# Feed-forward first, and attention with scores in row strips, probabilities scaled on Pool and turned in fp32, and fp32 values in column strips

## The chip, the cores and the metric

The kernel runs on one core of one Trainium2 chip. Its engines are TensorE (PE; PEld is its weight load), VectorE (DVE), ScalarE (ACT), GpSimd (Pool) and SyncE (SP, which here only issues DMAs). The metric is the device time of one execution in microseconds (us), lower is better. All times below are of this one core.

## The reference, cut to what matters

Input x is 8192 tokens of 512 numbers (fp32), in 64 blocks of 128 tokens.

```python
xn = layernorm(x)                                    # over the 512 numbers, no scale or shift
qkv = xn @ Wqkv + bqkv                               # 512 -> 1536; 16 heads of 32 numbers
scores = einsum('bhnqd,bhnkd->bhnqk', qb, kwin) / sqrt(512)   # a block sees itself and both neighbours
scores = where(|kpos - qpos| <= 128 and 0 <= kpos < 8192, scores, -1e30)
attn = softmax(scores)
attention = einsum('bhnqk,bhnkd->bhnqd', attn, vwin) @ Wout + bout
h = bitlinear(xn, w_fc) + gate * (xn @ v.T @ fast_b.T @ u.T)  # 512 -> 2048, weights rounded to -1, 0, 1 times a row scale
ffn = bitlinear(max(h, 0) ** 2, w_proj)                       # 2048 -> 512
out = x + attention + ffn
```

## The kernel before

Two stages run one after the other. `attention` writes x plus the attention result to a DRAM tensor `partial`; `feed_forward` reads x and `partial` and writes the output. Each engine has its own program, written out in a fixed order, and the engines meet at semaphores only. All loops are unrolled.

A product that must be close to fp32 is made of fp32r (rounded fp32) operands: each operand is split in a high part (a copy that rounds) and a low part (the rest), and three matmuls are added, high x high, low x high, high x low. `job_ps` holds such projections, two banks in turn.

**Attention** works on tiles of two blocks (256 tokens, 32 tiles). A tile has 32 steps (`STEPS`): c (4 groups of four heads) x b (2 blocks) x h (4 heads of the group). A step is one head of one query block against three key blocks, 128x384 scores. In step s PE makes, in this order: the scores of s (L913); a quarter of a projection, called a job (L290 for queries and keys, 256 columns each; L300 for values and L965 for the output projection, 512 columns each); the turn (transpose through PE) of the probabilities of step s-1 in three 128x128 pieces (L934), on some steps with a fourth, the rider (L931), which turns a piece of x or of the attention result; and every second step the products with the values of two earlier steps (L954, L956).

- Scores are one matmul with 96 rows: the three passes (high, high, low) of the 32 numbers of a head lie below each other in `stack`. ACT and DVE write the parts to `qk_parts` (L697 to L823), and SP copies them with 12 DMAs of 64 KB for each c (L544) to the other partitions.
- DVE adds the mask, scales and finds the maximum (`mask_scale_max`, L789). ACT takes the exponential (L716). PE turns the result, not yet divided by its sum. ACT copies the turned piece to fp16 (`pT_high`, L727), DVE makes the fp16 rest (`pT_low`, L800).
- The products with values take the turned probabilities (128x128) as weights and 97 or 65 columns of bf16 values: a column of ones for the row sum, the value's high, middle and low part. DVE adds the parts (`fold`, L813, L814), Pool multiplies by the reciprocal of the sum (L628).
- x is normalised and turned inside attention, and again in feed-forward.

**Feed-forward** first rounds, scales and turns the weights (`prepare_feed_forward`), then runs 16 tiles of 512 tokens in 16 steps: nine matmuls up (L1568 to L1572), eight down for two steps before (L1582, L1584), and on ACT and DVE relu, square, high part, low part. For the next tile it normalises x, turns it and splits it (`f_xT_hi`, `f_xT_lo`).

`prepare_attention` loads and splits the weights at the kernel's start. Between the blocks of the program all engines jump to new code and meet.

## Time and profile before

| | us |
|---|---|
| median of 3 runs | 2811.32 (2810.37 to 2813.68) |
| profiled execution, its own time | 2808.96 |
| its span, first to last instruction | 2807.0 |
| attention, up to the first DMA of feed-forward's weights | 1675.4 |
| feed-forward with its preparation | 1131.6 |

The median lies 2.36 us above the profiled execution's own time, and that lies 1.96 us above its span. An engine's busy time is the union of its instructions. A matmul's own duration contains the pipeline's depth, so what a matmul costs in a row of them is the distance from one start to the next, and not its duration; the same holds in part for ACT and DVE. PEclk 1.00 is TensorE's full clock, 2.4 GHz; 0.50 is 1.2 GHz.

### The profile page before, as it was taken

What the parts mean: (1) busy time and instruction counts of PE and PEld (TensorE: products, weight loads), DVE (VectorE), ACT (ScalarE), POOL (GpSimd) and SP (SyncE); (2) the same over time, 40 slices, a digit from 0 to 9 for tenths busy, and PEclk for the clock granted to TensorE, in tenths of its full rate; (3) what the DMA queues carried; (4) which work ended last, traced back from release to release, by engine and by line L of the source; (5) the groups of instructions that cost most, each with busy time, mean ns of one, the idle gap of its engine ahead of it and who ended that gap; (6) DMA issues with size and microseconds to landing.
All of it is one profiled execution on the core that took longest, in us unless ns stands there. A gap on an engine that the chain in (4) does not pass through costs nothing. (4 is left out here: it accounts for less than half of the span.)

```text
span 2807.0 us, 61651 instructions
## 1 busy us (share of the span) xinstructions
PE 2728.3 (97%) x20744; PEld 2397.7 (85%) x20744; DVE 2023.4 (72%) x5704; ACT 1712.8 (61%) x3745; POOL 639.1 (23%) x812
## 2 busy tenths in 40 slices
PE   6999999999999999999999977999999999999998
PEld 5899999999999999999999965888888888888887
DVE  4899999999999999999999966444444444444443
ACT  3678778787787877878778756333333333333332
POOL 3223323233233332323323220111111111111111
PEclk9999999999999999999999987999999999999999
DMA  3333333333333333333333333111111111111101
GB/s 114 92 97 93 99 94 105 89 92 100 95 98 96 94 99 94 99 94 94 99 95 95 97 90 137 49 46 49 45 50 46 49 46 45 46 45 46 45 31 45
DMA packets 177015, 219.98 MB, mean 78 GB/s; under 512 B 32112, under 2 KB 115280, under 8 KB 176192
## 3 DMA queue, kind: packets, MB, share of 16 engines
q1 hardware_dynamic: 175840, 215.31, 26.7%
q8 instruction: 170, 2.79, 0.4%
q14 instruction: 141, 1.16, 0.1%
q0 software_dynamic: 864, 0.73, 0.1%
HBM read 80.91 MB, written 33.55 MB: 41 GB/s over the span
## 5 line engine op out<-in xcount | busy, mean ns | idle before, releaser
L716 ACT ACTIVATE probs<-neg_scores,neg_max 128x384 f32<-128x384 f32 (+1 forms) x1024 | 630.8, 616 | 341.9 <-DVE neg_max L789 335.3
L789 DVE CUSTOM_DVE_ANT_0 neg_scores<-score_ps,mask 128x384 f32<-128x384 f32 (+1 forms) x1024 | 559.9, 547 | 109.0 <-PE score_ps L913 56.2
L1441 ACT ACTIVATE relu<-up_ps,fc_scale 128x512 f32<-128x512 f32 x256 | 176.3, 689 | 656.9 <-PE up_ps L1572 656.9
L800 DVE TENSOR_TENSOR pT_lo<-pT_ps,pT_hi 128x384 f16<-128x384 f32 (+1 forms) x1024 | 561.2, 548 | 13.5 <-ACT xT_hi L729 4.9
L1515 DVE SCALAR_TENSOR_TENSOR sq<-up_ps,relu 128x512 f32<-128x512 f32 x256 | 177.0, 691 | 536.2 <-ACT relu L1441 536.2
L934 PE MATMUL pT_ps<-ident,probs 128*128 128x128 f32 x3040 | 506.6, 275 | 12.4 <-ACT probs L716 9.8
L727 ACT CAST pT_hi<-pT_ps 128x384 f16<-128x384 f32 (+1 forms) x1024 | 470.1, 459 | 3.8 <-PE pT_ps L934 3.5
L913 PE MATMUL score_ps<-stack 96*128 96x128 f32 (+2 forms) x1536 | 448.9, 347 | 0.0
L934 PEld LDWEIGHTS pT_ps<-ident,probs 128*128 128x128 f32 x3040 | 366.0, 141 | 81.3 <-DVE oT_lo L804 12.9
L1582 PE MATMUL down_ps<-proj_T,sq_hi 128*128 128x512 f32 x1024 | 408.9, 399 | 0.3 <-DVE sq_lo L1498 0.2
L1584 PE MATMUL down_ps<-proj_T,sq_lo 128*128 128x512 f32 x1024 | 404.3, 395 | 0.0
L1568 PE MATMUL up_ps<-f_xT_hi,fc_T 128*128 128x512 f32 x1024 | 399.3, 390 | 1.4 <-DVE low L1486 1.4
L1570 PE MATMUL up_ps<-f_xT_lo,fc_T 128*128 128x512 f32 x1024 | 399.3, 390 | 0.0
L628 POOL TENSOR_TENSOR o_heads<-o_sum,o_rcp 128x128 f32<-128x128 f32 x256 | 102.3, 400 | 950.4 <-DVE o_sum L814 950.4
L290 PE MATMUL job_ps<-xT_hi,wqkv_hi 128*128 128x256 f32 x1024 | 295.5, 289 | 2.6 <-PEq L318 2.6
L954 PE MATMUL o_ps<-values,pT_hi 128*128 128x97 bf16 x3040 | 295.6, 208 | 0.2 <-DVE oT_lo L804 0.2
L956 PE MATMUL o_ps<-values,pT_lo 128*128 128x65 bf16 x3040 | 288.5, 194 | 0.0
L290 PE MATMUL job_ps<-xT_hi,wqkv_lo 128*128 128x256 f32 x1024 | 288.4, 282 | 0.0
L290 PE MATMUL job_ps<-xT_lo,wqkv_hi 128*128 128x256 f32 x1024 | 287.5, 281 | 0.0
L913 PEld LDWEIGHTS score_ps<-stack 96*128 96x128 f32 x1536 | 254.8, 193 | 0.1
L954 PEld LDWEIGHTS o_ps<-values,pT_hi 128*128 128x128 f16 x3040 | 251.5, 98 | 0.6 <-DVE oT_lo L804 0.4
L956 PEld LDWEIGHTS o_ps<-values,pT_lo 128*128 128x128 f16 x3040 | 239.0, 98 | 6.3
(165 smaller groups left out, 5186.1 us busy)
## 6 DMA issues: line engine op xcount, KB each, us to landing
stack<-qk_parts SPq DMA_DIRECT2D x1536, 64.0 KB, 2.1
x_in<-in_L_attn_x SPq DMA_DIRECT2D x64, 256.0 KB, 3.2
y<-in_L_attn_x SPq DMA_DIRECT2D x64, 256.0 KB, 3.0
partial<-y SPq DMA_DIRECT2D x64, 256.0 KB, 3.4
f_x_in<-in_L_attn_x SPq DMA_DIRECT2D x64, 256.0 KB, 2.7
part_in<-partial SPq DMA_DIRECT2D x64, 256.0 KB, 3.6
out<-f_y SPq DMA_DIRECT2D x64, 256.0 KB, 2.0
fc_in<-in_L_ffn_w_fc SPq DMA_DIRECT2D x16, 256.0 KB, 6.2
```

The lines of the kernel that those rows point to most:

```text
L290: last = nc.tensor.matmul(out, w[:, k, col:col + P], a[:, k, par, :] if is_k else own_tokens(a, par, k), start=(n == 0), stop=(n == 3 * DC ...
L716: nc.scalar.activation(probs[:, r, cols], neg_scores[:, r, cols], ACT.Exp, bias=neg_max[:, s % 4:s % 4 + 1], scale=-1.0).then_inc(probs_do ...
L727: last = nc.scalar.copy(pT_hi[:, s % 4, cols], pT_ps[:, r, cols])
L789: nc.vector.tensor_tensor_reduce(out=neg_scores[:, r, cols], in0=score_ps[:, r, cols], in1=mask[:, cols], scale=-SCORE_SCALE, scalar=3e38, ...
L800: last = nc.vector.tensor_tensor(pT_lo[:, s % 4, cols], pT_ps[:, r, cols], pT_hi[:, s % 4, cols], ALU.subtract)
L913: last = nc.tensor.matmul(score_ps[:, s % 2, (w - b) * P:(w - b + count) * P], q_cols(par, c, h, b), keys[:, at:at + count * P], start=Tru ...
L934: last = nc.tensor.transpose(pT_ps[:, r, w * P:(w + 1) * P], probs[:, r, w * P:(w + 1) * P], ident[:, :])
L954: nc.tensor.matmul(o_ps[:, g % 2, col:col + VW], pT_hi[:, r, t], v, start=(w == w0), stop=False)
L956: last = nc.tensor.matmul(o_ps[:, g % 2, col:col + 1 + 2 * DH], pT_lo[:, r, t], v[:, 0:1 + 2 * DH], start=False, stop=(w == w1 - 1))
L1568: nc.tensor.matmul(up_ps[:, s % 2, :], fc_T[:, k, cols], xT_hi[:, par, k, :], start=(k == 0), stop=False)
L1582: nc.tensor.matmul(down_ps[:, b, :], sq_hi[:, s % 2, t], proj_T[:, s, :], start=(s == 0), stop=False)
L1584: last = nc.tensor.matmul(down_ps[:, b, :], sq_lo[:, s % 2, t], proj_T[:, s, :], start=False, stop=(s == FB - 1))
```

## The change

- **Order of the stages.** `feed_forward_stage` runs first and writes x plus its result to `partial`. It also stores the turned, normalised x, high and low part, to a DRAM tensor `xT` (two DMAs of 256 KB for each block, `store_xT`). Its 14 middle tiles run in a hardware loop of seven passes instead of unrolled code. `attention_stage` then loads `xT` (four DMAs of 256 KB for each two blocks) and `partial`, and writes the output. It no longer normalises, turns or splits x.
- **Steps.** Attention now has 128 steps t (tile i, group c of four heads), each with all eight heads of two blocks. One t of the new kernel is the work of eight steps s of the old one.
- **Scores.** No `stack` and no DMAs of queries and keys. q and k, high and low, stay where the projection leaves them, four heads of 32 rows below each other. A head's three passes are three matmuls with 32 rows, placed in that head's row strip of the array (`tile_position=(h * DH, 0)`), the four heads after each other in each pass, each into its own bank of `score_ps`. Keys lie in a ring of four blocks; for every second tile a window wraps, and each pass is then two matmuls, 256 and 128 columns.
- **Softmax.** DVE still masks and finds the maximum, and writes to `probs`. ACT's exponential now also sums (`accum_out`). DVE takes four reciprocals at once, and Pool multiplies each head's 128x384 probabilities by them in place (`normalise`).
- **Turned probabilities.** PE turns as before. ACT copies each head's result to `pT` in fp32; there is no low part, so DVE has no part in it.
- **Values.** They are kept in fp32, one copy by ACT. The product takes a head's 32 columns of values as weights and the turned probabilities as moving data (fp32, 256 or 128 columns), each head in its own column strip (`tile_position=(0, h * DH)`). Its result is already turned, so the riders for the attention result go; ACT and DVE split it (`oT_high`, `oT_low`).

Core of the diff (`job_ps` now takes three jobs a step in two banks: A is the queries and keys of t+2, then the products with values of t-1, then B, values or output projection):

```diff
-def feed_forward(nc, x, partial, fast_b, w_fc, w_proj, u, v, gate, out):
+def feed_forward_stage(nc, x, fast_b, w_fc, w_proj, u, v, gate, xT_dram, partial):
...
-            for i in range(NT):
-                tile(i, i % 2)
+            tile(0, 0)
+            with eng.Fori(0, (NT - 2) // 2) as pair:
+                for n in range(2):
+                    tile(2 * pair + 1 + n, (1 + n) % 2)
+            tile(NT - 1, (NT - 1) % 2)
...
+            def store_xT(i, par):
+                for b in range(NB):
+                    sp.wait_ge(xT_done, NB * i + b + 1)
+                    settle(sp, ticks)
+                    for low, xT in enumerate((xT_hi, xT_lo)):
+                        sp.dma_start(xT_rows(xT_dram, NB * i + b, low),
+                                     xT[:, par, :, b * P:(b + 1) * P].bitcast(F32)).then_inc(xT_stored[b], 16)
...
+            def normalise(t, b):
+                i, _ = where(t)
+                cols = window(i, b)
+                pool.wait_ge(rcp_done, 2 * t + b + 1)
+                for h in range(HC):
+                    u = b * HC + h
+                    nc.gpsimd.tensor_scalar(probs[:, u, cols], probs[:, u, cols], sum_rcp[:, u:u + 1], None, ALU.mult
+                                            ).then_inc(normalised, 1)
...
+            def exp(t, b, h):
+                i, _ = where(t)
+                cols = window(i, b)
+                u = b * HC + h
+                act.wait_ge(maxed, 8 * t + u + 1)
+                nc.scalar.activation(probs[:, u, cols], probs[:, u, cols], ACT.Exp, bias=neg_max[:, u:u + 1], scale=-1.0,
+                                     accum_out=prob_sum[:, u:u + 1]).then_inc(exped, 1)
+            def copy_pT(t, b, h):
+                i, _ = where(t)
+                seen = blocks_seen(i, b)
+                first = 3 * at(i, b)
+                act.wait_ge(turned, 8 * t + b * HC + h + 1)
+                if t >= 1:
+                    act.wait_ge(pv_done, t)
+                nc.scalar.copy(pT[:, h, first + seen.start:first + seen.stop, :].rearrange("p w t -> p (w t)"),
+                               pT_ps[:, h % 2, seen.start * P:seen.stop * P]).then_inc(pT_done, 1)
...
+            def find_max(t, b):
+                i, _ = where(t)
+                cols = window(i, b)
+                dve.wait_ge(scored, 2 * t + b + 1)
+                if t >= 1:
+                    dve.wait_ge(turned, 8 * (t - 1) + HC * (b + 1))
+                for h in range(HC):
+                    u = b * HC + h
+                    nc.vector.tensor_tensor_reduce(out=probs[:, u, cols], in0=score_ps[:, h, cols], in1=mask[:, cols],
+                                                   scale=-SCORE_SCALE, scalar=3e38, op0=ALU.add, op1=ALU.min,
+                                                   accum_out=neg_max[:, u:u + 1]).then_inc(maxed, 1)
+            def invert_sums(t, b):
+                group = slice(b * HC, (b + 1) * HC)
+                dve.wait_ge(exped, 8 * t + HC * (b + 1))
+                nc.vector.reciprocal(sum_rcp[:, group], prob_sum[:, group]).then_inc(rcp_done, 1)
...
+            def scores(t, b):
+                i, c = where(t)
+                if b == 0:
+                    pe.wait_ge(qk_done, t + 1)
+                if t or b:
+                    pe.wait_ge(maxed, 8 * t + HC * b)
+                place = at(i, b)
+                for w, key, count in key_runs(i, b):
+                    for pass_ in range(PASSES):
+                        q = q_lo if pass_ == 1 else q_hi
+                        keys = k_lo if pass_ == 2 else k_hi
+                        for h in range(HC):
+                            rows = slice(h * DH, (h + 1) * DH)
+                            last = nc.tensor.matmul(
+                                score_ps[:, h, w * P:(w + count) * P], q[rows, c, place, :],
+                                keys[rows, c, key:key + count, :], start=(pass_ == 0), stop=(pass_ == PASSES - 1),
+                                tile_position=(h * DH, 0))
+                last.then_inc(scored, 1)
+            def turn_probs(t, b, h):
+                i, _ = where(t)
+                u = b * HC + h
+                n = 8 * t + u
+                if n >= 2:
+                    pe.wait_ge(pT_done, n - 1)
+                pe.wait_ge(normalised, n + 1)
+                for w in blocks_seen(i, b):
+                    last = nc.tensor.transpose(pT_ps[:, h % 2, w * P:(w + 1) * P], probs[:, u, w * P:(w + 1) * P],
+                                               ident[:, :])
+                last.then_inc(turned, 1)
+            def probs_times_values(t):
+                i, c = where(t)
+                bank = pv_bank(t)
+                wait_job_bank(pe, 3 * (t + 1) + 1)
+                if c == 0:
+                    pe.wait_ge(v_done, min(2 * i + 3, NBLK))
+                pe.wait_ge(pT_done, 8 * t + 2 * HC)
+                parts = []
+                for blk in (2 * i, 2 * i + 1):
+                    first, second = (3 * place + blk - (2 * i - 1 + at(i, place)) for place in range(2))
+                    parts.append((blk, slice(0, 2), slice(first, second + 1, second - first)))
+                for b, blk in enumerate((2 * i - 1, 2 * i + 2)):
+                    if 0 <= blk < NBLK:
+                        place = at(i, b)
+                        seen = 3 * place + 2 * b
+                        parts.append((blk, slice(place, place + 1), slice(seen, seen + 1)))
+                for n, (blk, places, seen) in enumerate(parts):
+                    for h in range(HC):
+                        head = c * HC + h
+                        strip = slice(h * DH, (h + 1) * DH)
+                        last = nc.tensor.matmul(job_ps[strip, bank, places.start * P:places.stop * P],
+                                                values[:, blk % VR, head * DH:(head + 1) * DH], pT[:, h, seen, :],
+                                                start=(n == 0), stop=(n == len(parts) - 1), tile_position=(0, h * DH))
+                last.then_inc(pv_done, 1)
...
+            for t in range(STEPS + 3):
+                if t < STEPS:
+                    scores(t, 0)
+                for part in range(QUARTERS):
+                    if 1 <= t <= STEPS:
+                        turn_probs(t - 1, 1, part)
+                    run_a(t, part)
+                if t < STEPS:
+                    scores(t, 1)
+                if 1 <= t <= STEPS:
+                    probs_times_values(t - 1)
+                for part in range(QUARTERS):
+                    if t < STEPS:
+                        turn_probs(t, 0, part)
+                    run_b(t, part)```

PE in the steady part of attention before: one step s, from its scores on, with a quarter of a query and key job and a rider. `stack` gives both operands of the scores, `o_ps` takes the products with values.

```order
L913 MATMUL score_ps<-stack 128x128
L913 MATMUL score_ps<-stack 128x256
L290 MATMUL job_ps<-xT_hi,wqkv_hi 128x256
L290 MATMUL job_ps<-xT_lo,wqkv_hi 128x256
L290 MATMUL job_ps<-xT_hi,wqkv_lo 128x256
L290 MATMUL job_ps<-xT_hi,wqkv_hi 128x256
L290 MATMUL job_ps<-xT_lo,wqkv_hi 128x256
L290 MATMUL job_ps<-xT_hi,wqkv_lo 128x256
L931 MATMUL pT_ps<-ident,o_heads 128x128
L934 MATMUL pT_ps<-ident,probs 128x128 x3
```

PE now, in the middle of a step t: the end of job A, the scores of the second block, the products with values of the step before, then the first turn of this step.

```order
L1135 MATMUL job_ps<-xT_hi,wqkv_lo 128x256
L1200 MATMUL score_ps<-k_hi,q_hi 128x384 x4
L1200 MATMUL score_ps<-k_hi,q_lo 128x384 x4
L1200 MATMUL score_ps<-k_lo,q_hi 128x384 x4
L1238 MATMUL job_ps<-pT,values 32x256 x8
L1238 MATMUL job_ps<-pT,values 32x128 x8
L1214 MATMUL pT_ps<-ident,probs 128x128 x3
L1144 MATMUL job_ps<-wqkv_hi,xT_hi 128x512
```

The scores of four heads now stand together, and the products with values are 16 instructions of 32 output rows in place of 48 with 97 and 65 columns.

ACT before, in the same part: exponential and fp16 copy in turn, two casts of riders, the projection's high parts.

```order
L716 ACTIVATE probs<-neg_scores,neg_max 128x384
L727 CAST pT_hi<-pT_ps 128x384
L729 CAST oT_hi<-pT_ps 128x128
L716 ACTIVATE probs<-neg_scores,neg_max 128x384
L727 CAST pT_hi<-pT_ps 128x384
L729 CAST oT_hi<-pT_ps 128x128
L697 ACTIVATE qk_parts<-job_ps,qk_bias 128x256
L699 ACTIVATE qk_parts<-job_ps,qk_bias 128x256
```

ACT now, from the last exponential of a step's first block on.

```order
L985 ACTIVATE probs,prob_sum<-probs,neg_max 128x384
L1011 ACTIVATE q_hi<-job_ps,qk_bias 128x256
L1014 ACTIVATE k_hi<-job_ps,qk_bias 128x256
L985 ACTIVATE probs,prob_sum<-probs,neg_max 128x384
L1003 CAST oT_hi<-job_ps 128x256
L995 COPY pT<-pT_ps 128x384
L985 ACTIVATE probs,prob_sum<-probs,neg_max 128x384
L995 COPY pT<-pT_ps 128x384
```

The copy behind an exponential is now that of a head four places back, and between a head's exponential and its copy lie DVE's reciprocal, Pool's scaling and PE's turn.

## Rows read from the trace of the kernel before

**Rows 1.** The page's busy times: us, share of the span, number of instructions.

```profile
PE 2728.3 (97%) x20744; PEld 2397.7 (85%) x20744; DVE 2023.4 (72%) x5704; ACT 1712.8 (61%) x3745; POOL 639.1 (23%) x812
```

**Rows 2.** Stretches of attention's steady part: all engines; ACT's exponentials alone.

```profile
500.00:1000.00 500.00, 498.87 (x4944) 463.02 (x4942) 463.94 (x1456) 397.47 (x936) 155.77 (x200) 1.00 0.36 96
500.00:1000.00 500.00, 197.62 (x319) 1.00 0.36 96
```

**Rows 3.** Who waited for whom from 500 to 1000: us in total, times, longest.

```profile
ACT probs L716 <- DVE neg_max L789: 100.2, 210, 1.4
PEld pT_ps L934 <- DVE oT_lo L804: 3.3, 15, 0.3
```

**Rows 4.** Timeline of PE: start us, us, line, op; one wrapped step, values behind.

```profile
805.92 0.21 PE L954 MATMUL o_ps<-values,pT_hi 128*128 128x97 bf16 x1
...
806.36 0.48 PE L913 MATMUL score_ps<-stack 96*128 96x128 f32 x2
806.67 0.40 PE L300 MATMUL job_ps<-wqkv_hi,xT_hi 128*128 128x512 f32 x1
806.91 0.39 PE L300 MATMUL job_ps<-wqkv_hi,xT_lo 128*128 128x512 f32 x1
```

**Rows 5.** The same timeline, a step with a query and key job.

```profile
812.65 0.42 PE L913 MATMUL score_ps<-stack 96*128 96x384 f32 x1
812.91 0.28 PE L290 MATMUL job_ps<-xT_hi,wqkv_hi 128*128 128x256 f32 x1
813.03 0.28 PE L290 MATMUL job_ps<-xT_lo,wqkv_hi 128*128 128x256 f32 x1
...
813.62 0.49 PE L934 MATMUL pT_ps<-ident,probs 128*128 128x128 f32 x3
813.86 0.42 PE L913 MATMUL score_ps<-stack 96*128 96x384 f32 x1
```

**Rows 6.** Timeline of PE and its weight loads: fp32 products of 512 and 128 columns; fp32r of 128.

```profile
25.85 0.19 PEld L188 LDWEIGHTS bias_ps<-wout_raw,v_bias_wide 128*128 128x128 f32 x1 [0.24 <-issue]
26.28 0.19 PEld L188 LDWEIGHTS bias_ps<-wout_raw,v_bias_wide 128*128 128x128 f32 x1 [0.24 <-issue]
1723.74 1.06 PE L1225 MATMUL scale_ps<-diagonal,ones 128*128 128x128 f32 x8
31.50 0.28 PE L379 MATMUL job_ps<-xT_hi,wqkv_hi 128*128 128x128 f32 x1
31.61 0.28 PE L379 MATMUL job_ps<-xT_lo,wqkv_hi 128*128 128x128 f32 x1
```

**Rows 7.** Timeline of ACT: attention's pair of a step; a sum's read behind an activation.

```profile
806.35 0.46 ACT L727 CAST pT_hi<-pT_ps 128x384 f16<-128x384 f32 x1
806.71 0.60 ACT L706 CAST values<-job_ps 128x512 bf16<-128x512 f32 x1
1683.41 0.19 ACT L1243 ACTIVATION_READ_ACCUMULATOR absolute<-fc_in 128x1 f32 x1
1683.50 0.67 ACT L1261 ACTIVATE fc_T<-turn_ps,neg_round 128x512 fp32r<-128x512 f32 x1
```

**Rows 8.** Groups by shape: line, engine, op, count | busy us, mean ns | idle before.

```profile
L716 ACT ACTIVATE probs<-neg_scores,neg_max 128x384 f32<-128x384 f32 x992 | 614.5, 619 | 323.0 <-DVE neg_max L789 316.5
L789 DVE CUSTOM_DVE_ANT_0 neg_scores<-score_ps,mask 128x384 f32<-128x384 f32 x992 | 546.5, 551 | 101.1 <-PE score_ps L913 50.0 <-ACT probs L716 26.9 <-issue 0.8
L642 POOL TENSOR_TENSOR y<-y,projected 128x512 f32<-128x512 f32 x64 | 82.4, 1288 | 3.1 <-ACT projected L746 3.1
L614 POOL CAST values<-v_rest 128x512 bf16<-128x512 f32 x64 | 39.9, 623 | 157.5 <-DVE v_rest L830 157.5
```

**Rows 9.** Timeline at borders: first projection, first scores, first weight DMA of feed-forward.

```profile
28.35 0.47 PE L300 MATMUL job_ps<-wqkv_hi,xT_hi 128*128 128x512 f32 x1 [1.05 <-PEq L79]
39.33 0.55 PE L290 MATMUL job_ps<-xT_hi,wqkv_hi 128*128 128x256 f32 x1 [2.64 <-PEq L318]
1675.40 7.50 SPq L1095 DMA_DIRECT2D fc_in<-in_L_ffn_w_fc  x10
```

**Rows 10.** The page's DMA issues: count, KB each, us to landing; and a burst's rate (last number, GB/s).

```profile
x_in<-in_L_attn_x SPq DMA_DIRECT2D x64, 256.0 KB, 3.2
1680.00:1700.00 20.00, 14.75 (x54) 9.70 (x55) 14.33 (x55) 15.95 (x39) 0.00 (x0) 0.50 1.02 376
```

1242 lines of the change are left out of this document (444 added, 798 removed).

## The prediction

> **What bounds the kernel now.** I read the busy times first [rows 1]: PE is busy for 97% of the span, DVE 72%, ACT 61%, Pool 23%. Then attention's steady part [rows 2]: in 500 us PE is busy for 498.9 at the full clock, DVE for 463.9 (93%), ACT for 397.5 (79%), Pool for 155.8. The 319 exponentials there are 319 old steps, so eight of them, the work of one new step t, take 500 / 319 x 8 = 12.54 us. Waits [rows 3]: ACT waits often for DVE's maxima, but for PE's weight loads the worst releaser comes to 3.3 us in 500. PE sets the pace, and attention gains only what PE gains, until another engine takes over.
>
> What the 12.54 are made of, by the distance from one start to the next. A job's matmul of 256 columns takes 0.118 (six in 0.71 [rows 5]), one of 512 takes 0.24 [rows 4]: 24 x 0.118 + 12 x 0.24 = 5.72. Turns: three in 0.24 [rows 5], eight times 1.92. Riders: four more turns, 0.32. Scores: 0.26 with one run of keys [rows 5], 0.31 with two [rows 4], half of each: 2.28. Products with values: 12 matmuls, two steps, in 0.44 [rows 4], four times 1.76. Sum 12.00; 0.54 are gaps.
>
> **What PE does per new step.** The jobs (5.72) and the 24 turns (1.92) stay. The four riders go (-0.32). Two terms have no row, since no matmul of before shares the array with another.
>
> Scores. A column costs 0.118 / 256 = 0.46 ns, so a pass of 384 columns 0.175. Lower bound: the four strips run beside each other, a block costs three passes and what a waiting start costs (0.26 - 0.175 = 0.09) and about as much on leaving the strips: 0.70, wrapped 3 x (0.118 + 0.11) + 0.19 = 0.87, the 0.11 being the distance of 128-column matmuls, whose weight loads set the pace [rows 6]. Two blocks, half of the tiles wrapped: 1.6 us. Upper bound: nothing overlaps, 12 x 0.175 + 0.1 and wrapped 12 x 0.228 + 0.1, per step 5.0. I take 1.6: neighbours in the order lie in different rows, read different partitions and write different banks.
>
> Values. An fp32 product is two loads and two matmuls: the weight loads of the 512-column one start 0.43 apart, the eight records of four 128-column ones 0.11 apart [rows 6]. A half is so 0.215 for 256 columns and 0.11 for 128. Upper bound, nothing overlaps: 8 x 0.43 + 8 x 0.22 + 0.1 = 5.3. Lower bound, four strips at once: 2 x 0.43 + 2 x 0.22 + 0.1 = 1.4. I take a value between, for a reason in the order: the two halves of a head follow each other in the same strip, so the second waits for the first, and in a queue that starts matmuls in order the next head can only begin beside that second half. Two run at a time, not four: 8 x 0.215 + 8 x 0.11 + 0.1 = 2.7.
>
> Sum: 5.72 + 1.92 + 1.6 + 2.7 = 11.94. Of the 0.54 gaps I keep 0.2 (the values' four short runs and the riders, which wait on DVE, are gone), within 0.1 to 0.54. **12.14 us** against 12.54.
>
> The Trainium skill (TensorE: Matmul & The Clock Gate, Part 3, Packing small matmuls) gives measured gains of 3.07 times for four row strips and 2.38 for three column strips. By these the two terms would be 5.0 / 3.07 = 1.6 and 5.2 / 2.38 = 2.2, the step about 11.6 us and the kernel some 2710 us, an estimate from that page. No run here shows it yet.
>
> **Does the rest keep up?** ACT: of a 0.46 copy the next start comes after 0.36 [rows 7], so I take 0.10 off each duration. Exponential 0.62 - 0.10 [rows 8], plus a sum's read that puts off the next start by 0.09 [rows 7]: 0.61, eight times 4.9. Copies 8 x 0.36 = 2.9. Query and key parts 2 x 0.38, the result's high part 0.26, half a value copy 0.25: together 9.1 us. It loses the riders' casts and x, and gains the reads. DVE: 8 x 0.48 for the maxima (0.55 [rows 8], overlapped in part), query and key rests 0.8, 0.4 for the result's rest, reciprocals 0.2, half of an output addition 0.35: 5.6 us. `pT_low`, `fold` and x go; they are beside PE's work and save nothing themselves. Pool: no row has its new operation. Bounds: one input, 512 columns, 0.62; two inputs, 1.29 [rows 8]; so 0.47 to 0.97 for 384, eight times 3.8 to 7.8, plus half of 1.29. I take 0.6, nearer to the one-input row. All are below 12.1.
>
> The chain across engines, for the second block of a step: its last exponential, a sum's read, a reciprocal (0.18), Pool (0.47 to 0.97), three hops of about 0.1, then the first turn of the next step. I lay the orders out from the start of the first block's scores. They end at 0.8, job A with the old block's turns at 4.6, the second scores at 5.4, values at 8.1, job B with turns at 12.1. DVE takes the first maxima from 1.1 to 3.1, but the second only after the rests of queries and keys, which wait for job A and for four exponentials on ACT: from 7.4. ACT's exponentials of the second block then start at 8.0 and the last ends at 11.7. The first turn of the next step is wanted at 12.9; with Pool at 0.6 it is free at 12.7, with 0.97 at 13.1. So the chain just fits: cost 0 to 0.3 us a step, 0 taken. Were PE faster, it would be the bound: with values at 1.4 the same table closes at 11.3, since ACT then runs behind PE's turns.
>
> **Outside the steady part.** Before, attention takes 1675.4 us to feed-forward's first DMA [rows 9], less 128 x 12.54: 70 fixed. Now: weights as before until 27; no x beside them, so that eight loads of 256 KB (2.1 MB at 376 GB/s, 3.2 us to landing [rows 10]) stand on the path, 8; the opening projections 48 x 0.11 + 24 x 0.24 + 48 x 0.118 = 17 with 3 of waits; last step's values, two output projections and the store 18. 73, so +3. Feed-forward's arithmetic does not change. SP there issues eight stores of x's parts more in each tile of some 66 us, 2.1 MB or 32 GB/s; attention held 96 [rows 2]. SP's next load of x stands behind those stores, issued by step 10 of 16, and is wanted in step 1 of the next tile: some 20 us. The loop's seven jumps back: jumps to new code cost PE 1.05 and 2.64 [rows 9], with engines meeting; queued matmuls may hide them. 0 to 18 us, 7 taken. The Pool and SP queues lose value carrying and 1536 stack DMAs, which nobody on PE waited for.
>
> **Sum.** 128 x (12.14 - 12.54) = -51; +3; +7. Span 2807 - 41 = 2766, plus 1.96 outside it and 2.36 to the median: **2770 us**. Gaps and bounds of these terms (11.9 to 12.5 a step, 0 to 25 outside) give 2733 to 2831 for this case.
>
> **Rivals.**
> - *All four column strips overlap too.* For: they are different columns, and each reads its own head. Against: the two halves of a head in one strip. The chain closes at 11.3: 2811 + 10 - 128 x 1.24 = 2662.
> - *One kind of strip does not overlap* (slower). Place: in the scores each matmul has its own 128-column weight load, and loads pass one at a time, 0.11 apart, as [rows 6] may be read: 12 or 24 a block, 4.2 us a step. Or the column strips run in turn, 5.3. Either gives a step of 14.7: 2811 + 10 + 128 x 2.2 = 3100. It decides from the point where scores and values together cost over 4.6 us against my 4.3.
> - *Neither overlaps.* 18.2 a step, about 3545.
> - *The chain bites.* Pool at 0.97 or longer hops, turns waiting at each step's start: 12.4 to 12.9 a step, 2803 to 2868, middle 2835.
>
> **How the numbers follow.** Forecast 0.36, full overlap 0.18, one kind not 0.27, neither 0.05, chain 0.14. A measurement tells about 0.2%, 6 us, from no change. Faster: 0.33 of the forecast's share, 0.18, 0.03 of the chain's: 0.54. Same 0.05, slower 0.41. Both signs hold much, so the forecast's own range, 2733 to 2831, stands beside the range 2662 to 3110, which leaves out "neither" and the edges.
>
> **What would show it.** Steady PE rows: starts of the four heads' score matmuls within hundredths of a us and a block in 0.7 to 0.9; values 2.7 a step, with two heads' halves beside each other; PE over 97% busy and a step 12.1. The chain shows as PE's weight loads of the turns waiting for Pool; its row is 0.47 to 0.97 long. A score block of 1.3 or more is the queue of loads. I am wrong by a lot if strips don't share the array; a little if the loop's jumps or Pool cost more.

## The result, and the profile after

The changed kernel takes 2876.8 us (2876.1 to 2879.4) where the kernel before, run beside it, takes 2811.3: a ratio of 1.0233, interval 1.0215 to 1.0251. It is slower by 65 us; 2770 were forecast. The profiled execution has a span of 2873.4 us, so 66 more than before.

The busy times of the changed kernel's page answer to [rows 1]: us, share of the span, number of instructions. Under them stand two stretches of attention's steady part, all engines (PE, PEld, DVE, ACT, POOL, then PEclk, DMA share, GB/s) and the exponentials' line alone, which answer to [rows 2].

```profile
PE 2734.9 (95%) x21264; PEld 2110.3 (73%) x21264; DVE 1276.2 (44%) x3777; ACT 1667.3 (58%) x4261; POOL 1452.6 (51%) x1234
```

```profile
1300.00:1800.00 500.00, 485.58 (x4935) 360.90 (x4934) 224.34 (x829) 369.04 (x1055) 399.96 (x326) 1.00 0.14 40
```

```profile
1300.00:2300.00 1000.00, 437.18 (x1226) 1.00 0.14 42
```

A step has eight exponentials and eight reads of their sums, so 1226 records in 1000 us are 1000 / 1226 x 16 = **13.05 us per step**, against 12.54 before and 12.14 forecast. No engine looks full: DVE fell to 45%, PE is at 97%, Pool, which had 31%, is at 80% of the stretch. PE's 97% mislead here: a matmul's modelled end covers short pauses, and the number of its records says more (4935 in 500 us at 13.05; 5554 in a version below that takes 11.56).

The rest of the span is as forecast. Rows of the border between the stages:

```profile
1130.01 1.26 POOL L456 TENSOR_TENSOR f_y<-f_y,part_in 128x512 f32<-128x512 f32 x1
...
1133.85 1.94 SPq L689 DMA_DIRECT2D w_stage<-in_L_attn_Wqkv  x4
```

Feed-forward and its border take 1133.85 us against 1131.6, and attention 2873.4 - 1133.85 = 1739.6, of which 128 x 13.05 = 1670.4 are steps and 69 are fixed (73 forecast). The whole loss is in the step.

**Where the step goes.** The groups of Pool and PE between 1300 and 2800 us (count | busy us, mean ns | idle before, releaser), and the waits between 1500 and 2500 us (us in total, times, longest), which answer to [rows 8] and [rows 3]:

```profile
L956 POOL TENSOR_SCALAR probs<-probs,sum_rcp 128x384 f32<-128x384 f32 x920 | 1128.2, 1244 | 300.1 <-DVE sum_rcp L1063 300.1
L1214 PE MATMUL pT_ps<-ident,probs 128*128 128x128 f32 x2760 | 479.0, 283 | 43.4 <-POOL probs L956 42.8
```

```profile
DVE sum_rcp L1063 <- ACT probs L985: 446.8, 153, 3.7
POOL probs L956 <- DVE sum_rcp L1063: 199.1, 153, 2.1
...
ACT pT L995 <- PE pT_ps L1214: 114.0, 77, 1.9
```

Pool's product takes 1.244 us for 384 columns, always (1240 to 1255 ns over 920 of them), above the upper bound of 0.97. Eight make 9.95 us, and half an output addition of 1.28 brings Pool to 10.6 of 13.05. The rest is in the second list: Pool stands still for DVE's reciprocals, twice a step, 199.1 us in 1000 or 2.6 a step. The timelines of Pool, ACT and DVE through one step show the ring:

```profile
1999.30 3.69 POOL L956 TENSOR_SCALAR probs<-probs,sum_rcp 128x384 f32<-128x384 f32 x3
2002.95 1.28 POOL L961 TENSOR_TENSOR y<-y,out_bias 128x512 f32<-128x512 f32 x1
2005.08 4.91 POOL L956 TENSOR_SCALAR probs<-probs,sum_rcp 128x384 f32<-128x384 f32 x4 [0.85 <-DVE sum_rcp L1063]
2011.12 2.46 POOL L956 TENSOR_SCALAR probs<-probs,sum_rcp 128x384 f32<-128x384 f32 x2 [1.13 <-DVE sum_rcp L1063]
```

```profile
2003.69 0.48 ACT L995 COPY pT<-pT_ps 128x384 f32<-128x384 f32 x1
2004.06 0.62 ACT L985 ACTIVATE probs<-probs,neg_max 128x384 f32<-128x384 f32 x1
...
2006.91 0.62 ACT L985 ACTIVATE probs<-probs,neg_max 128x384 f32<-128x384 f32 x1 [1.41 <-DVE neg_max L1056]
...
2010.09 0.64 ACT L985 ACTIVATE probs<-probs,neg_max 128x384 f32<-128x384 f32 x1
```

```profile
2005.53 0.48 DVE L1075 SCALAR_TENSOR_TENSOR q_lo<-job_ps,qk_bias,q_hi 128x256 fp32r<-128x256 f32 x1 [0.55 <-ACT k_hi L1014]
...
2006.32 0.55 DVE L1056 CUSTOM_DVE_ANT_0 probs<-score_ps,mask 128x384 f32<-128x384 f32 x1
```

Pool ends the old block's fourth head at 2002.99 (the old block is the second block of the step before). Only then can PE turn it and ACT copy it (2003.69), and only behind that copy, in ACT's order, stands the fourth exponential of the new step's first block (2004.06). Two things hang on it.

- DVE inverts the first block's four sums in one instruction (2004.80), and Pool begins that block at 2005.08: 2.09 us after it was done, in which the output addition fits on half of the steps. It ends at 2009.99.
- ACT's query and key parts stand behind the same exponential, DVE's rests wait for them (2005.53), and the second block's maxima stand behind the rests (2006.32). So ACT starts the second block's exponentials at 2006.91, one for each copy between them, and the fourth at 2010.09. The single reciprocal waits for that fourth one, and Pool begins the second block at 2011.12, 1.13 after it was free.

For Pool the step is 8 x 1.23 + 2.09 + 1.13 = 13.06. The ring that sets it is the second way: from the end of the old block's four products to the start of the second block's 8.13 us pass on PE, ACT and DVE, and the four products themselves take 4.91, together 13.04. Pool waits for itself. The first block's products lie beside this ring, with the 1.13 behind them.

**The strips**, the part of the forecast with no row, overlap at least as well as forecast. PE's timeline of one block's scores, the values and the next turn:

```profile
2004.29 0.45 PE L1200 MATMUL score_ps<-k_hi,q_hi 32*128 32x384 f32 x4
2004.57 0.34 PE L1200 MATMUL score_ps<-k_hi,q_lo 32*128 32x384 f32 x4
2004.74 0.34 PE L1200 MATMUL score_ps<-k_lo,q_hi 32*128 32x384 f32 x4
2005.01 1.51 PE L1238 MATMUL job_ps<-pT,values 128*32 128x256 f32 x32
2006.47 0.53 PE L1214 MATMUL pT_ps<-ident,probs 128*128 128x128 f32 x3
```

A block of scores takes 2005.01 - 2004.29 = 0.72, the values 1.46. Line L1238 alone in slices of 0.05 us shows how many of its records run:

```profile
2005.00:2005.05 0.05, 0.04 (x4) 1.00 0.00 0
...
2005.20:2005.25 0.05, 0.05 (x4) 1.00 0.72 287
2005.25:2005.30 0.05, 0.05 (x8) 1.00 1.47 573
```

Four records start together and the next four 0.2 us later: all four heads, half by half, side by side.

### The profile page after: what moved, and what is told of

It is laid out like the page before. It is cut to its first block, busy times and chain, and to the rows that moved or that the text cites. A ratio compares the mean times of both kernels' runs of the same rounds, so it can differ in the third digit from the quotient of the medians.

```text
span 2873.4 us, 58706 instructions
## 1 busy us (share of the span) xinstructions
PE 2734.9 (95%) x21264; PEld 2110.3 (73%) x21264; DVE 1276.2 (44%) x3777; ACT 1667.3 (58%) x4261; POOL 1452.6 (51%) x1234
## 4 chain that ended last, share of the span: by engine, by line
PE 20%; ACT 19%; issue 9%; POOL 6%; DVE 5%; SPq 0%; DMA 0%; ACTq 0%; POOLq 0%
ACT probs L985 10%; PE job_ps L1135 10%; PE pT_ps L1214 9%; POOL probs L956 6%; ACT pT L995 5%; DVE probs L1056 2%; DVE k_lo L1079 2%; ACT k_hi L1014 2%; ACT q_hi L1011 2%; ACT oT_hi L1003 1%; DVE sum_rcp L1063 1%; PE job_ps L1250 0%; PE job_ps L1153 0%; PE job_ps L1144 0%; SPq L921 0%
## 5 line engine op out<-in xcount | busy, mean ns | idle before, releaser
L956 POOL TENSOR_SCALAR probs<-probs,sum_rcp 128x384 f32<-128x384 f32 (+1 forms) x1024 | 1245.4, 1234 | 398.3 <-DVE sum_rcp L1063 398.3
L985 ACT ACTIVATE probs<-probs,neg_max 128x384 f32<-128x384 f32 (+1 forms) x1024 | 633.3, 618 | 180.0 <-DVE neg_max L1056 180.0
L995 ACT COPY pT<-pT_ps 128x384 f32<-128x384 f32 (+1 forms) x1024 | 486.6, 475 | 249.5 <-PE pT_ps L1214 199.8
L1214 PE MATMUL pT_ps<-ident,probs 128*128 128x128 f32 x3040 | 532.1, 284 | 64.1 <-POOL probs L956 60.0
L1214 PEld LDWEIGHTS pT_ps<-ident,probs 128*128 128x128 f32 x3040 | 315.7, 141 | 321.9 <-issue 244.0
L1056 DVE CUSTOM_DVE_ANT_0 probs<-score_ps,mask 128x384 f32<-128x384 f32 (+1 forms) x1024 | 504.0, 548 | 80.2 <-PE score_ps L1200 78.6
L456 POOL TENSOR_TENSOR f_y<-f_y,part_in 128x512 f32<-128x512 f32 x64 | 87.4, 1397 | 665.1 <-DVE f_y L561 665.1
L1063 DVE RECIPROCAL sum_rcp<-prob_sum 128x4 f32<-128x4 f32 x256 | 45.5, 178 | 751.5 <-ACT probs L985 751.5
L1135 PE MATMUL job_ps<-xT_hi,wqkv_hi 128*128 128x256 f32 x1024 | 330.3, 323 | 0.0
L1135 PE MATMUL job_ps<-xT_lo,wqkv_hi 128*128 128x256 f32 x1024 | 287.3, 281 | 0.0
L1135 PE MATMUL job_ps<-xT_hi,wqkv_lo 128*128 128x256 f32 x1024 | 286.4, 280 | 0.0
L637 PEld LDWEIGHTS down_ps<-proj_T,sq_hi 128*128 128x128 f32 x1024 | 193.4, 189 | 42.8 <-DVE sq_lo L553 1.1
L639 PEld LDWEIGHTS down_ps<-proj_T,sq_lo 128*128 128x128 f32 x1024 | 193.0, 188 | 43.1
L623 PEld LDWEIGHTS up_ps<-f_xT_hi,fc_T 128*128 128x128 f32 x1024 | 192.3, 188 | 43.9 <-DVE low L541 2.0
L625 PEld LDWEIGHTS up_ps<-f_xT_lo,fc_T 128*128 128x128 f32 x1024 | 192.3, 188 | 42.5
L985 ACT ACTIVATION_READ_ACCUMULATOR probs<-probs,neg_max 128x1 f32 x1024 | 199.2, 195 | 0.0
## 6 DMA issues: line engine op xcount, KB each, us to landing
xT_hi<-xT SPq DMA_DIRECT2D x66, 256.0 KB, 3.9
xT_lo<-xT SPq DMA_DIRECT2D x66, 256.0 KB, 4.4
f_x_in<-in_L_attn_x SPq DMA_DIRECT2D x64, 256.0 KB, 3.2
xT<-f_xT_hi SPq DMA_DIRECT2D x64, 256.0 KB, 2.6
xT<-f_xT_lo SPq DMA_DIRECT2D x64, 256.0 KB, 2.8
part_in<-in_L_attn_x SPq DMA_DIRECT2D x64, 256.0 KB, 3.6
partial<-f_y SPq DMA_DIRECT2D x64, 256.0 KB, 2.0
ff_in<-partial SPq DMA_DIRECT2D x64, 256.0 KB, 3.4
```

Of the source, the lines that this page charges most:

```text
L623: nc.tensor.matmul(up_ps[:, s % 2, :], fc_T[:, k, cols], xT_hi[:, par, k, :], start=(k == 0), stop=False)
L625: nc.tensor.matmul(up_ps[:, s % 2, :], fc_T[:, k, cols], xT_lo[:, par, k, :], start=False, stop=False)
L637: nc.tensor.matmul(down_ps[:, b, :], sq_hi[:, s % 2, t], proj_T[:, s, :], start=(s == 0), stop=False)
L639: last = nc.tensor.matmul(down_ps[:, b, :], sq_lo[:, s % 2, t], proj_T[:, s, :], start=False, stop=(s == FB - 1))
L956: nc.gpsimd.tensor_scalar(probs[:, u, cols], probs[:, u, cols], sum_rcp[:, u:u + 1], None, ALU.mult).then_inc(normalised, 1)
L985: nc.scalar.activation(probs[:, u, cols], probs[:, u, cols], ACT.Exp, bias=neg_max[:, u:u + 1], scale=-1.0, accum_out=prob_sum[:, u:u + 1] ...
```

## The experiments

All shorten or lengthen one thing in the changed kernel or in a version of it. A step's length is read as above, from the exponentials' records. Experiments 1, 7, 8 and 11 change what the kernel computes and have one run each; the differences read from them are far above the 0.2% by which runs of one kernel differ. The edits are shortened: conditions around calls are left out, and nested loops stand in one line.

**1. Without the scaling.** The output lacks the division by the sums.

```
-                    normalise(t, 0)
-                    normalise(t, 1)
...
-                pe.wait_ge(normalised, n + 1)
+                pe.wait_ge(exped, n + 1)
```

> The changed kernel with Pool's scaling of the probabilities left out (the turn waits for the exponential instead; the result is attention without the division by the row sum). Theory: Pool's 1.24 us instruction paces the turns, and a step is 8 x 1.23 plus Pool's two waits of 2.09 and 1.13 us, 13.03 together. Without it the chain of the prediction's table is left, 11.3 us a step, span about 2873 - 128 x 1.7 = 2655. Rival one, the orders written out on ACT and PE cost the same with a cheap scaling: a step stays above 12.5, span above 2805. Rival two, PE itself is full (its matmuls behind a turn start late): a step of 12.5 to 13, PE still 97% busy.

2682.0 us. Its stretch and its exponentials:

```profile
1300.00:1800.00 500.00, 500.00 (x5536) 415.18 (x5533) 250.54 (x934) 407.15 (x1189) 28.35 (x22) 1.00 0.16 48
```

```profile
1300.00:2300.00 1000.00, 493.47 (x1384) 1.00 0.16 48
```

16000 / 1384 = 11.56 us per step, PE never idle. The scaling costs 1.5 us a step, which is the whole loss of 0.5 and 1.0 more; PE's own work is 11.56, where the forecast had 12.14.

**2. VectorE scales instead of Pool**, four products behind each reciprocal.

```
-normalise(t, 0)
-normalise(t, 1)
...
 nc.vector.reciprocal(sum_rcp[:, group], prob_sum[:, group]).then_inc(rcp_done, 1)
+for h in range(HC):
+    nc.vector.tensor_scalar(probs[:, u, cols], probs[:, u, cols], sum_rcp[:, u:u + 1], None, ALU.mult)
```

> The changed kernel with the same scaling on DVE, right behind the four reciprocals. DVE has 5.6 us of work in a step of 13.0; the instruction should take 0.40 to 0.48 us (a 128x512 tensor_scalar with a scalar from memory took 0.487 before), so DVE has 9 us. It delays DVE's second maxima by 1.6 us at most. Theory: a step of 11.5 to 12.4, median 2680 to 2800. Rival, the chain through DVE takes over: with the second maxima at 9.0 and not 7.4 in the table the step comes to 12.9, median about 2860.

2861.1 us, ratio 1.0179 (1.0162 to 1.0196). The product takes DVE 0.42 us instead of Pool's 1.24, and it brings only 16 us. DVE's timeline:

```profile
2003.50 0.18 DVE L1060 RECIPROCAL sum_rcp<-prob_sum 128x4 f32<-128x4 f32 x1 [2.20 <-ACT probs L982]
2003.72 1.41 DVE L1065 TENSOR_SCALAR probs<-probs,sum_rcp 128x384 f32<-128x384 f32 x4
2005.04 0.68 DVE L1092 TENSOR_TENSOR y<-job_ps,ff_in 128x512 f32<-128x512 f32 x1
2005.64 0.55 DVE L1053 CUSTOM_DVE_ANT_0 probs<-score_ps,mask 128x384 f32<-128x384 f32 x1
```

The next block's maxima stand behind the four products (and an output addition), ACT's exponentials wait for the maxima, and the next reciprocal for the exponentials. DVE then idles for 2.2 us, in a step in which it is 65% busy. It is a ring again, through other stations.

**3. Pool's product in its two-input form**, the reciprocal repeated along the row.

```
-nc.gpsimd.tensor_scalar(probs[:, u, cols], probs[:, u, cols], sum_rcp[:, u:u + 1], None, ALU.mult
+nc.gpsimd.tensor_tensor(probs[:, u, cols], probs[:, u, cols],
+                        sum_rcp[:, u:u + 1].to_broadcast([P, n_]), ALU.mult
```

> The changed kernel with Pool's tensor_scalar replaced by a tensor_tensor whose second input is the reciprocal spread over the columns. The prediction's upper bound came from Pool's two-input rows, 2.5 ns a column, 0.97 us for 384; the tensor_scalar took 3.2 ns a column. If that row holds for this form, a step is 8 x 0.97 + 3.2 = 11.0 to 11.3, median about 2650 to 2690. Rival: Pool pays for the in-place work on this tile or for its neighbours DVE and ACT, whatever the instruction: 1.2 us again and no change, 2877.

2755.2 us, ratio 0.9801 (0.9785 to 0.9817): some 2% below the kernel before, by this line alone.

```profile
L957 POOL TENSOR_TENSOR probs<-probs,sum_rcp 128x384 f32<-128x384 f32 x941 | 748.6, 827 | 594.0 <-DVE sum_rcp L1065 594.0
```

With two inputs read the product takes 0.83 us, a third less than with one. The step is now 16000 / 1328 = 12.05 us. It did not reach the 2650 to 2690 expected: Pool, 58% busy, still waits, and the products behind the first no longer set the distance of the turns. PE's own order does:

```profile
2004.15 0.49 PE L1216 MATMUL pT_ps<-ident,probs 128*128 128x128 f32 x3
...
2005.18 0.49 PE L1216 MATMUL pT_ps<-ident,probs 128*128 128x128 f32 x3
```

A turn with its quarter of a job takes 1.03. So the ring is 8.13 + 0.83 + 3 x 1.03 = 12.05, an estimate from the rows of both kernels that meets the measured step.

**4. All four exponentials of the first block ahead of the old block's copies.**

```
-for h in range(HC): copy_pT(t - 1, 1, h); exp(t, 0, h)
+for h in range(HC): exp(t, 0, h)
+for h in range(HC): copy_pT(t - 1, 1, h)
```

> The changed kernel with ACT's order alone changed: the four exponentials of a step's first block ahead of the four copies of the block before, in place of turn and turn about. Theory: Pool's wait of 2.09 us between blocks is there because the last exponential stands behind a copy that waits for Pool's own last result; with it gone Pool has 8 x 1.23 + 0.64 + the other wait of 1.1 = 11.6 us a step, median about 2877 - 128 x 1.4 = 2700, Pool over 85% busy. Rival, Pool's length alone matters: a step stays at 12.8 to 13.0, since the copies now come late to PE: 2845 to 2880.

2890.8 us, ratio 1.028 (1.0263 to 1.0297), slower still, and the theory falls in this form. Two waits from 1500 to 2500 us, and ACT's first copies of one step:

```profile
DVE q_lo L1076 <- ACT k_hi L1014: 258.9, 76, 3.4
...
PE pT_ps L1215 <- ACT pT L995: 40.1, 76, 0.7
```

```profile
2009.83 0.83 ACT L995 COPY pT<-pT_ps 128x384 f32<-128x384 f32 x2
```

The longest wait is DVE's, for ACT's query and key parts (`qk_high`), which now stand behind the fourth copy; in the changed kernel it is 41.9 us in 76 times. By the chain that the profile follows back, the step's length does not come from it. That chain goes through PE: the old block's third turn waits for its first copy (the turned pieces have two banks), that copy stands behind four exponentials, they wait for the new block's first maximum (1993.71), and the next first maximum (2006.83) waits for PE's order from that third turn on. That is 13.1 us, and no product of Pool is in it. Opening one way round closed another. This is read from the trace; no run tests it.

**5. A reciprocal for each head.** Neither Pool's instruction nor any order is changed; only the wait is cut into four.

```
-dve.wait_ge(exped, 8 * t + HC * (b + 1))
-nc.vector.reciprocal(sum_rcp[:, group], prob_sum[:, group]).then_inc(rcp_done, 1)
+for u in range(b * HC, (b + 1) * HC):
+    dve.wait_ge(exped, 8 * t + u + 1)
+    nc.vector.reciprocal(sum_rcp[:, u:u + 1], prob_sum[:, u:u + 1]).then_inc(rcp_done, 1)
...
-pool.wait_ge(rcp_done, 2 * t + b + 1)
+pool.wait_ge(rcp_done, 8 * t + u + 1)     # ahead of each head's product
```

> Pool scales as in the changed kernel, 1.244 us a head, but VectorE inverts each head's sum as soon as that head's exponentials are there (four small reciprocals in a block of queries instead of one behind the fourth head), and Pool waits for each head by itself. Nothing else is changed. Theory A, it is the wait and not the length of Pool's instruction: in the changed kernel Pool stands idle for 2.1 and 1.1 us between its two blocks of four, because the last exponentials stand on ScalarE behind copies that wait for Pool itself. With the wait cut to a head, Pool works through: 8 x 1.24 + half of 1.28 = 10.6 us per step, less than TensorE's 11.56 without scaling, so 11.6 to 11.9 us per step and 2690 to 2730 us. Theory B, the length decides: turns 1.24 apart within a block, PE idle there, cannot be caught up; 13.0 us per step and 2870 us.

**2684.8 us, ratio 0.9549** (0.9533 to 0.9565). Pool's product is as slow as before, 1250 ns, and the step is 16000 / 1384 = 11.56 us, that of the kernel without scaling. Its stretch, and Pool's timeline:

```profile
1300.00:1800.00 500.00, 500.00 (x5554) 414.96 (x5547) 284.22 (x1192) 406.64 (x1186) 451.47 (x368) 1.00 0.16 48
```

```profile
2002.27 1.29 POOL L961 TENSOR_TENSOR y<-y,out_bias 128x512 f32<-128x512 f32 x1
2003.52 4.93 POOL L956 TENSOR_SCALAR probs<-probs,sum_rcp 128x384 f32<-128x384 f32 x4
2008.81 4.92 POOL L956 TENSOR_SCALAR probs<-probs,sum_rcp 128x384 f32<-128x384 f32 x4 [0.35 <-DVE sum_rcp L1063]
```

Pool is 90% busy and ahead of PE. With the product as long as before, cutting the wait for the fourth head gives back the whole loss. Pool need no longer wait from the second block's first exponential to its fourth, 2010.09 - 2006.91 = 3.2 us, so that the ring is some 9.9 us, an estimate from those rows, and PE's 11.56 is longer. Against the kernel before it brings 127 us.

**6. VectorE scales, interleaved**: product, maximum, product, maximum, head by head, and the query and key rests behind the first product.

```
 invert_sums(t, 0)
+scale(t, 0, 0)
 qk_low(job_a(t), a_bank(t))
-find_max(t, 1)
+find_max(t, 1, 0); scale(t, 0, 1); find_max(t, 1, 1); scale(t, 0, 2)
 oT_low(t - 1)
-invert_sums(t, 1)
+find_max(t, 1, 2); scale(t, 0, 3); find_max(t, 1, 3)
```

> VectorE scales, as in the run that took 2861 us, but its work is in another order: the sums of one block and the maxima of the next are interleaved head by head (scale, maximum, scale, maximum), where before four scalings stood in one piece (1.32 us) ahead of the four maxima that ScalarE waits for. Theory A: the 2861 us came from a closed ring of VectorE and ScalarE (reciprocal, four scalings, low parts of the keys, maximum, then four exponentials and copies 0.97 us apart, and round again), not from VectorE's total, which is 7.8 us in a step of 12.9. In this order the ring is open and TensorE sets the step at 11.56 us: 2685 to 2710 us. Theory B, VectorE's scalings and ScalarE's exponentials can't keep up in any order: 2800 us or more.

2700.1 us, ratio 0.9602 (0.9585 to 0.9618), against 2861 with the same instructions in the other order (the second block's sums are inverted at the start of the next step). The ring of experiment 2 was DVE's order. The reciprocal is still one for four heads here: with a product of 0.42 us and this order that wait no longer sets the pace, so cutting it is one way to open the ring and not the only one.

**7. A constant for the reciprocal** (every probability is multiplied by 0.01 and none divided by its sum).

```
-... probs[:, u, cols], sum_rcp[:, u:u + 1], None, ALU.mult
+... probs[:, u, cols], 0.01, None, ALU.mult
```

> Pool multiplies by the number 0.01 written in the instruction instead of by each row's reciprocal; the probabilities are therefore wrongly scaled (the sums are left out of the product), nothing else is changed. If reading the factor from memory makes Pool's one-input instruction slow, it drops from 1.244 us to about 0.8 (the two-input form with a broadcast reciprocal took 0.83) or below, and the time to 2690 to 2755 us. If the one-input form is slow by itself, it stays at 1.24 us and 2875 us.

2835.4 us, between the two that were expected; Pool's product takes 1170 ns. Reading a factor for each row costs 0.07 of the 1.24; the rest of the price is there with a constant too. Of Pool's eight products the ring holds four: 128 x 4 x 0.074 = 38 us, and 41 were gained.

**8. Heads outermost**, on the kernel without scaling (the output lacks the division).

```
-for pass_ in range(PASSES): for h in range(HC):
+for h in range(HC): for pass_ in range(PASSES):
...
-for n, (blk, places, seen) in enumerate(parts): for h in range(HC):
+for h in range(HC): for n, (blk, places, seen) in enumerate(parts):
```

> The kernel without scaling (Pool's product left out, so the probabilities are not divided by their sums; that took 2682 us and 11.56 us per step, with TensorE never idle), and in scores and values the loop over heads is put outermost, so that matmuls that follow each other share a strip and can't run side by side. It prices the overlap of strips. In the changed kernel the twelve matmuls of a block's scores take about 0.85 us and the thirty-two records of the values 1.45. In one strip: scores 12 x 0.16 = 1.9 us or more a block (384 columns by the rate of the projections, 256 in 0.118), the prediction's bound was 2.5; values 16 matmuls at 4 passes over 128 and 256 columns, the prediction's bound was 5.3 a step. So 11.56 + 2 x (1.9 to 2.5 less 0.85) + (5.3 less 1.45), 17.5 to 18.7 us per step, 3440 to 3600 us. If the overlap is not what makes these stages short, 11.6 and 2682.

3013.9 us. PE's timeline around a wrapped block of scores, and around the values:

```profile
2005.26 0.41 PE L1197 MATMUL score_ps<-k_hi,q_hi 32*128 32x256 f32 x4
2005.48 0.31 PE L1197 MATMUL score_ps<-k_hi,q_lo 32*128 32x256 f32 x4
...
2006.12 0.55 PE L1211 MATMUL pT_ps<-ident,probs 128*128 128x128 f32 x3
...
2011.32 3.95 PE L1235 MATMUL job_ps<-pT,values 128*32 128x256 f32 x30
```

```profile
2015.42 0.55 PE L1211 MATMUL pT_ps<-ident,probs 128*128 128x128 f32 x3
```

The values take 2015.42 - 2011.32 = 4.10 us instead of 1.46. That is the whole difference, 128 x 2.64 = 338 us (measured 332). The heads do not quite follow one another. Line L1235 in two slices, before and after the second head begins (how many records run):

```profile
2012.15:2012.20 0.05, 0.05 (x2) 1.00 0.00 0
...
2012.45:2012.50 0.05, 0.05 (x5) 1.00 0.00 0
```

A head's eight records take 4 x 0.216 + 4 x 0.109 = 1.30 us by the distances of their starts (0.215 and 0.11 in the forecast), but the second head begins 0.89 after the first, beside its four short ones. With no overlap at all the four heads would take 5.2, an estimate from these. The scores still take 0.86, and their records still start four at a time, pass by pass, though the program now has head 0's three passes ahead of head 1's first. Row strips ran beside each other in either order of the program; column strips did so in full only when neighbours in the order lay in different strips, and for a third of a head otherwise.

**9. Pool's two-input form on top of experiment 5.**

```
+pool.wait_ge(rcp_done, 8 * t + u + 1)
+nc.gpsimd.tensor_tensor(... sum_rcp[:, u:u + 1].to_broadcast([P, n_]), ALU.mult
```

> The version with a reciprocal for each head (2684.8 us) with Pool's product in the two-input form, 0.83 us instead of 1.25 us a head. Theory A, with the wait cut to a head TensorE alone sets the step: Pool's 33% shorter instruction brings nothing, 2680 to 2690 us. Theory B, the length of Pool's instruction still costs: 2640 to 2670 us.

2679.9 us, ratio 0.9548 (0.9523 to 0.9573) against 0.9549 in experiment 5, the step again 16000 / 1385 = 11.55. With the ring open a third off Pool's product is worth nothing that can be measured; with it closed (experiment 3) it was worth 121 us.

**10. Turns in pairs**, on top of experiment 9.

```
 turn_probs(t, 0, part)
+turn_probs(t, 0, part + 1)
 run_b(t, part)
+run_b(t, part + 1)
...
 copy_pT(t - 1, 1, h)
+copy_pT(t - 1, 1, h + 1)
 exp(t, 0, h)
+exp(t, 0, h + 1)
```

> As the run beside it (two-input product, reciprocal for each head), and TensorE turns two heads in a row and then does two quarters of a job; ScalarE copies and exponentiates two heads in a row likewise. Four of the eight changes from turns to job matmuls in a step go. In the traces the first job matmul behind a turn starts 0.25 us after the turn and the next one 0.20 us later, where job matmuls are otherwise 0.118 apart: 0.085 us per change. Theory A, these 0.085 us are TensorE's own and every change removed gives them back: 4 x 0.085 x 128 = 44 us less, 2641 us. Theory B, ScalarE (3.9 us for four exponentials and four copies against some 4.0 us for the four turns and the job) now stands in the way, since its copies come in pairs behind two exponentials: 2680 to 2750 us.

2722.2 us, ratio 0.9681 (0.9667 to 0.9695), 16000 / 1347 = 11.88 a step. PE's timeline of one pair:

```profile
2001.37 0.82 PE L1220 MATMUL pT_ps<-ident,probs 128*128 128x128 f32 x6
2001.95 0.37 PE L1141 MATMUL job_ps<-xT_hi,wqkv_hi 128*128 128x256 f32 x1
2002.15 0.28 PE L1141 MATMUL job_ps<-xT_lo,wqkv_hi 128*128 128x256 f32 x1
```

Six turns take 0.58, and the job's second matmul comes 0.085 late again: 0.58 + 0.085 is six times 0.11. So the 0.085 is no price of changing from turns to jobs. A turn of 128 fp32 columns costs 0.11, three cost 0.33, and the row that shows three in 0.24 holds the first part of them only. Nothing was to be gained, and with ACT's pairs PE's weight loads wait for a copy, 42.0 us in 84 steps, 0.5 a step; in experiment 9 it was 8.3.

**11. All scores in one row strip**, on top of experiment 5 (the scores of heads 1 to 3 are those of head 0).

```
-rows = slice(h * DH, (h + 1) * DH)
+rows = slice(0, DH)
...
-tile_position=(h * DH, 0)
+tile_position=(0, 0)
```

> The version with a reciprocal for each head (2684.8 us, 11.56 us per step, TensorE never idle), in which the scores of all four heads are computed with the rows of head 0 alone, in one row strip (the scores of heads 1 to 3 are therefore those of head 0; the number and size of the matmuls are the same). Prices the overlap of row strips, which the order of the matmuls did not touch. If four strips run at once and one strip runs its twelve matmuls one after the other, a block's scores go from 0.85 to 12 x 384 columns by 0.118 us for 256 = 2.1 us: 2 x 1.3 = 2.5 us more per step, 14.1 and 3005 us. If the strips do not matter, 2685 us.

3221.0 us. PE's timeline, one block:

```profile
2010.11 0.96 PE L1200 MATMUL score_ps<-k_hi,q_hi 32*128 32x384 f32 x4
2010.92 0.85 PE L1200 MATMUL score_ps<-k_hi,q_lo 32*128 32x384 f32 x4
2011.61 0.85 PE L1200 MATMUL score_ps<-k_lo,q_hi 32*128 32x384 f32 x4
2012.40 0.55 PE L1214 MATMUL pT_ps<-ident,probs 128*128 128x128 f32 x3
```

Twelve passes take 2.29 instead of 0.73, and a wrapped block 2.96 (0.86): four row strips give a factor of 3.1 to 3.4. Two blocks, half of them wrapped, are 5.25 us against 1.6. That explains 3.6 us of the 4.2 by which the step grew (16000 / 1014 = 15.8). The granted clock of the stretch was 0.96, 4% of 15.8 or 0.6 us, which fits the rest.

**12. Feed-forward's loop written out**, on top of experiment 5.

```
-with eng.Fori(0, (NT - 2) // 2) as pair:
-    for n in range(2):
-        tile(2 * pair + 1 + n, (1 + n) % 2)
+for i in range(NT):
+    tile(i, i % 2)
```

> The version with a reciprocal for each head, with the feed-forward part's loop of hardware written out for all token tiles; nothing else is changed. The prediction put 7 us (0 to 18) on the jumps of this loop. In the traces the feed-forward part ends within 1 us of where it did in the kernel before. Theory A, the jumps cost nothing because each engine runs ahead of the one that limits: 2680 to 2690 us. Theory B, each jump costs its engine some tenths of a us: 2667 to 2680 us. A third case: instructions written out must be loaded, and that costs more than the jumps: above 2690 us.

2685.8 us (2684.6 to 2686.4) against 2684.8 (2683.4 to 2686.2) with the loop. The jumps cost nothing that can be measured.

## Why the prediction was wrong, step by step

Its sum, with what was measured: 2766 of span; the step +128 x (13.05 - 12.14) = +116; attention's fixed part -4; feed-forward -5; together 2873, the span measured.

- **Pool's product, 0.6 us within 0.47 to 0.97.** The first step that failed. It is 1.244. Both bounds were rows of other operations (a cast, a two-input addition), picked by the number of inputs. The same product with two inputs takes 0.83, so the number of inputs does not order these costs.
- **"The chain across engines just fits, cost 0 to 0.3."** The second failure, and the one that decides. The table followed the chain once, from the second block to the next step's first turn, with Pool as one link of 0.6. It had the query and key parts, the second maxima and the fourth exponential of the second block in it. It left out what leads back: the first block's fourth exponential, on which the query and key parts stand, is itself behind a copy that waits for Pool's fourth product of the step before. That closes a ring in which four of Pool's products stand in a row, and the single reciprocal keeps the first of them behind a fourth exponential. Cutting that wait to a head brings 192 us with Pool as slow as ever (experiment 5). Moving the product to DVE without cutting the wait leaves 2861 in one order (experiment 2) and 2700 in another (experiment 6). Even at the forecast's 0.6 us the ring would be 8.13 + 0.6 + 3 x 1.03 = 11.8, an estimate from the rows, and so above PE's 11.56: the way back alone costs 0.3 a step, and the product's real price the other 1.2. The rival "the chain bites" named the right place (Pool, turns waiting) with a chance of 0.14, but ended at 2868, since it took Pool at 0.97 and had no way back.
- **Scores, 1.6 us.** Right: 0.73 and 0.88, 1.6 a step. The upper bound, 5.0 with no overlap, is 5.25 (experiment 11). The page of the Trainium skill (TensorE: Matmul & The Clock Gate, Part 3, Packing small matmuls) gives 3.07 for four row strips, and the traces agree, with 3.1 for whole blocks and 3.4 for wrapped ones.
- **Values, 2.7 us.** Wrong, 1.46. The reason given, halves of a head that follow each other in a strip and hold back the next head, is refuted by the records, which start four at a time; and matmuls in different strips do not start in the program's order (experiment 8). The lower bound, 1.4, was the value. The upper bound, 5.3 with no overlap, agrees with four times a head's 1.30 (experiment 8), so the factor is 3.6 for four column strips. The same section of the Trainium skill has 2.38 for three; no run here has three.
- **Turns 1.92 and gaps 0.2.** Too low together by 0.7: turns are 24 x 0.11 = 2.64. The three that the row shows in 0.24 have 0.09 of their cost behind them, as a late second matmul (experiment 10). In the kernel before, the matmul behind the turns was that of the scores, and the 0.09 stood in its 0.26 [rows 5]; with the scores it was taken out of the sum, though the turns stayed. PE's true sum is 5.72 + 2.64 + 1.6 + 1.46 = 11.4, and 0.15 of gaps give the 11.56 of experiments 1, 5 and 9. The errors in values and in turns and gaps cancel by half: 12.14 was wrong by 0.6 as PE's sum.
- **Loop jumps, 7 us.** They cost none (experiment 12), and feed-forward with its border grew by 2.2. The rest, ACT 9.1 and DVE 5.6, kept below PE as forecast: in experiment 1 ACT is 81% busy and DVE 50%.
- **The rivals.** "All column strips overlap" had the right PE, and its 2662 would be 2685 with the turns at their price; but it took the chain to close at 11.3, with Pool at 0.6. The two on strips that do not overlap, 0.32 together, did not come true. The wide range, 2662 to 3110, held the time only because these stood for slower, which is luck; the forecast's own, 2733 to 2831, did not. (Its lower edge follows from 11.9 a step with 3 us outside, not 0.)

## What to carry to other kernels

When work is handed to another engine, follow the handing on round to the same engine one block later: if one hop waits for the last of a group and another engine's order puts the new block's last item behind the old one's, the group's whole duration stands in the ring and no engine needs to be full for it to set the pace. Try to cut such a wait to one item before making an instruction faster; here four small reciprocals instead of one turned +2.3% into -4.5%, and made the speed of Pool's product irrelevant. An operation that has no row on its engine deserves a bound wider than its neighbours by operand count, and the price in time should be given for that wide bound as well.

## What the runs showed of the hardware

- GpSimd multiplies 128x384 fp32 by a factor for each row in 1.244 us, by a constant in 1.170, and by a second tensor, which is the factor repeated along the row, in 0.827. VectorE does the first in 0.416. The addition of 512 columns on GpSimd takes 1.288 (2.5 ns a column, against 2.2 and 3.2 for the products).
- Four row strips of fp32r matmuls overlapped to a factor of 3.1 to 3.4 whether the program named them pass by pass or head by head. Four column strips of fp32 products overlapped in full (1.46 us) only when named block by block, and took 4.10 head by head, where each head began 0.89 us after the one before and needed 1.30 itself. The two differ in strip direction and in type, and no run separates these, so which of them makes the order matter stays open.
- A turn of 128 fp32 columns costs 0.11 us, of which three in a row before a job matmul show 0.24 to 0.25 together and the other 0.085 as a late second matmul.
